# A four-layer network on one core: attention weights times values in one part of sixteen, a fourth weights buffer, the end in halves, and a new table of orders

## The reference, cut to what matters

```python
q, k: 16 heads of 32; v: 8 heads of 64
dots = einsum('bhqd,bhkd->bhqk', q, k)
attn_w = softmax(dots, axis=-1).reshape(B, H, 2, T, T)
attn_w = attn_w[:, :, 0] - lam * attn_w[:, :, 1]
attn = einsum('bhqk,bhkd->bhqd', attn_w, v)
...
rms = sqrt(mean(attn * attn, axis=-1, keepdims=True))
attn = gamma * (attn / (rms + EPS)) * (1.0 - LAMBDA_INIT)
return attn.transpose(0, 2, 1, 3).reshape(B, T, 2 * H * D) @ Wout
```

## Time and profile before

| what | value |
|---|---|
| runs: median (lowest, highest) of 3 | 2716.16 us (2714.27, 2717.32) |
| the profiled execution's own time | 2715.86 us |
| its span, first to last instruction | 2713.5 us |
| granted TensorE clock, mean over the span | 0.898 |
| busy in the span: PE, DVE, ACT, POOL | 79%, 77%, 64%, 57% |
| attention stage | 1026.5 to 2064 us of the span |

### The profile page before, as it was taken

How to read it: one execution, slowest core, us unless ns; L and a number is a source line. 1 busy time by engine, 2 the same in 40 slices (tenths; PEclk the granted TensorE clock), 3 DMA queues, 4 the chain that set the end, 5 groups by cost and what they waited for, 6 DMA issues and landing times.

```text
span 2713.5 us, 42415 instructions
## 1 busy us (share of the span) xinstructions
PE 2148.9 (79%) x15570; PEld 1464.3 (54%) x15570; DVE 2101.5 (77%) x3554; ACT 1741.9 (64%) x2750; POOL 1547.5 (57%) x1375
## 2 busy tenths in 40 slices
PE   2433896797696997898989898889996699769886
PEld 1101564465364674565666566556664568546675
DVE  6999899899886218999999999999998432762344
ACT  6443886786674538898888888888894234222432
POOL 1545335434534006788877987898788524673156
PEclk7555898899798998999999999999998899879988
DMA  2000000000000101111101110111110000000000
GB/s 115 0 0 0 1 1 1 1 1 20 1 1 1 24 1 24 25 25 25 26 23 30 29 27 21 28 24 25 24 36 24 1 1 1 1 16 1 1 1 16
DMA packets 22093, 42.22 MB, mean 16 GB/s; under 512 B 6528, under 2 KB 7040, under 8 KB 21504
## 3 DMA queue, kind: packets, MB, share of 16 engines
q1 hardware_dynamic: 21888, 39.52, 5.5%
HBM read 12.23 MB, written 2.10 MB: 5 GB/s over the span
## 4 chain that ended last, share of the span: by engine, by line
PE 36%; DVE 29%; issue 13%; ACT 12%; POOL 10%; DMA 0%; POOLq 0%; ACTq 0%; DVEq 0%
DVE MA L1326 12%; PE ps L888 6%; DVE WB L1335 5%; PE ps L817 3%; ACT HR L789 3%; PE ps L1187 2%; PE ps L1158 2%; PE ps L819 2%; PE ps L818 2%; PE ps L2048 2%; ACT BIG L455 2%; PE ps L1170 2%; POOL MA L421 2%; PE ps L1990 2%; ACT L789 1%
## 5 line engine op out<-in xcount | busy, mean ns | idle before, releaser
L1326 DVE TENSOR_REDUCE MA<-ps 128x1 f32<-128x1024 f32 x512 | 606.5, 1215 | 43.9 <-PE ps L1158 39.5
L1254 ACT ACTIVATE WB<-ps,MA 128x1024 f32<-128x1024 f32 x461 | 513.3, 1117 | 107.7 <-DVE MA L1326 95.9
L421 POOL TENSOR_TENSOR MA<-MA,BIG 128x1024 f32<-128x1024 f32 x128 | 303.1, 2388 | 475.0 <-DVE BIG L343 450.5
L1158 PE MATMUL ps<-BIG 96*128 96x512 f16 x1024 | 314.1, 389 | 100.7 <-ACT WB L1254 90.1
L1410 POOL TENSOR_SCALAR WB<-WB,MA 128x384 f32<-128x384 f32 x256 | 370.7, 1448 | 8.5
L888 PEld LDWEIGHTS ps<-WB,HR 128*128 128x128 f32 x2304 | 273.5, 192 | 32.4 <-issue 10.5
L888 PE MATMUL ps<-WB,HR 128*128 128x128 f32 x2304 | 282.4, 278 | 9.6 <-DVE acc L724 9.6
L1766 POOL TENSOR_TENSOR BIG<-MA,BIG 128x512 f32<-128x512 f32 x128 | 133.2, 1048 | 237.1 <-PE ps L2034 87.1
L789 ACT ACTIVATE HR<-ps,second 128x512 f32<-128x512 f32 x288 | 189.7, 686 | 113.4 <-PE ps L819 112.4
L1170 PE MATMUL ps<-first,WB 128*128 128x128 f32 x1640 | 225.7, 282 | 1.1 <-ACT WB L1261 0.4
L1413 POOL TENSOR_TENSOR WB<-WB 128x384 f32<-128x384 f32 x205 | 209.1, 1020 | 17.1
(11 more groups left out here) (314 smaller groups left out, 4933.2 us busy)
## 6 DMA issues: line engine op xcount, KB each, us to landing
BIG<-BIG SPq DMA_DIRECT2D x192, 64.0 KB, 2.0
BIG<-MA SPq DMA_DIRECT2D x192, 64.0 KB, 2.0
WB<-w_dram SPq DMA_DIRECT2D x1, 2304.0 KB, 15.0
X<-x_dram SPq DMA_DIRECT2D x4, 512.0 KB, 16.2
HR<-w_dram SPq DMA_DIRECT2D x1, 2048.0 KB, 9.6
out_dram<-X SPq DMA_DIRECT2D x4, 512.0 KB, 2.6
BIG<-wqkv_dram SPq DMA_DIRECT2D x1, 1536.0 KB, 6.2
WB<-w_dram SPq DMA_DIRECT2D x2, 512.0 KB, 5.1
```

What stands on the lines that cost most here:

```text
L421: e.tensor_tensor(yy[:, c, :], yy[:, c, :], db[n % 2][c], ALU.add).then_inc(*p_my.up(b, n, c))
L1158: x = e.matmul(ps[s][:, 512 * h:512 * h + 512], stack[q % 2][0:96, 0, 2 * pp + s, 128 * i:128 * i + 128], stack[q % 2][0:96, 1, 2 * pp + s ...
L1254: e.activation(P_of(n, s), ps[s][:, :], ACT.Exp, bias=L[:, 2 * s + pp:2 * s + pp + 1], scale=1.0, accum_out=L[:, 4 + 2 * s + pp:5 + 2 * s ...
L1326: e.tensor_reduce(L_of(n)[:, c:c + 1], ps[s][:, :], AX, ALU.max, negate=True).then_inc(*v_amx.up(n, s))
```

## The change

It makes no arithmetic different. It has five parts.

1. `weigh0` emits nothing, and `weigh1` emits all sixteen products of a pair and carries the one semaphore increment. `t_aw` has one tick per pair.
2. The second map gets a fourth buffer. It lies in a tile `spread` of 128 x 1024; `combT`, which had 9 partitions of its own, becomes its first nine.
3. The end of a round is a stream of its own (`end_dve`, `end_pool`) in halves of four tiles: the first half may start after step 7 of the last experts. `store` writes 256 KB pieces.
4. `LATE` has a number for each kind of piece instead of `between`, and for some steps one number for even units and one for odd.
5. All tables of due times get new numbers (`IN_AT0` to `A_AT`, `LATE`, `D_AT`; not shown, except for `LATE`).

```diff
+        spread = sb("spread", [128, 1024])
+        combT = spread[0:9, :]
...
-        LATE = {"pe": {"scores1": -0.12, "flip0": -0.01, "flip1": -0.37, "weigh0": 0.71, "weigh1": 0.06,
-                       "settle": 0.03, "between": -0.22},
+        LATE = {'pe': {'scores0': (-0.07, 0.08), 'scores1': (-0.11, 0.05), 'flip0': (-0.16, -0.18), 'flip1': (-0.29, -0.34), 'weigh0': 0.73, 'weigh1': -0.01, 'settle': 0.02, 'norm': -0.22, 'turn': -0.33, 'op': -0.26, 'v': -0.03, 'a3': -0.17, 'a4': -0.23},
...
-              [WB[:, 1024 * i:1024 * i + 1024] for i in range(3)]]
+              [WB[:, 1024 * i:1024 * i + 1024] for i in range(3)] + [spread[:, :]]]
...
-                if part == 0:
+                if part == 1:
                     e.wait_ge(*a_at.at(n))
...
-                for k in range(4 * part, 4 * part + 4):
+                for k in range(8 * part):
                     for pp in range(2):
                         x = e.matmul(bank[6][64 * pp:64 * pp + 64, 0:128], V[(4 * b + g) % 2][:, k, 64 * pp:64 * pp + 64],
                                      DT[(2 * m + pp) % 4][:, 128 * k:128 * k + 128], start=k == 0, stop=k == 7)
-                x.then_inc(*t_aw.up(m, part))
+                if part:
+                    x.then_inc(*t_aw.up(m))
...
+        def end_dve(e, k):
+            for r in range(2):
+                hs = (s_hs[k], s_hs1[k])[r]
+                for h in range(2):
+                    tiles, s = hs[:, 4 * h:4 * h + 4, :], st[f"d{k}"][:, 4 * h:4 * h + 4, :]
+                    yield end_at(k, r, h, "end_stats")
+                    stats(e, s, [tiles[:, j, :] for j in range(4)], {0: p_dm[k].at(r, 8 * h + 7)}).then_inc(
+                        *v_dend[k].up(r, h, "stats"))
+                    yield end_at(k, r, h, "end_norm")
+                    e.wait_ge(*p_dend[k].at(r, h))
+                    norms(e, s, [tiles[:, j, :] for j in range(4)], tiles, range(4)).then_inc(*v_dend[k].up(r, h, "out"))
```

More of the change, by code:

```diff
@@ L290, in rstd @@
             e.wait_ge(*pool_own.now())
-            return e.tensor_tensor(s[:, 0:n, 9:10], s[:, 0:n, 8:9], half_col[0], ALU.pow)
+            return e.tensor_tensor(s[:, 0:n, 9:10], s[:, 0:n, 8:9], half_col[0][:, 0:n, :], ALU.pow)
         def stats(e, s, src, ready):
-            for j in range(8):
+            for j in range(len(src)):
                 if j in ready:
@@ L996, in at @@
                 t, p = ORDER[x]
-                what = p[0] + str(p[2]) if p[0] in ("scores", "flip", "weigh") else p[0] if p[0] in UNIT_AT else "between"
-                return round(t + LATE[engine].get(what, 0), 3) if p[0] != "end" else t
+                late = LATE[engine].get(p[0] + str(p[2]) if p[0] in ("scores", "flip", "weigh") else p[0], 0)
+                if isinstance(late, tuple):
+                    late = late[p[1] % 2]
+                return round(t + late, 3) if p[0] != "end" else t
             return [(at(x), ORDER[x][1]) for x in sorted(range(len(ORDER)), key=lambda x: (at(x), x))]
@@ L1484, in program @@
         a_dg = two("a_dg", *keys(16))
-        v_dln = two("v_dln", *keys((2, 3), ("stats", "out")))
+        v_dln, v_dend = two("v_dln", *keys((2,), ("stats", "out"))), two("v_dend", *keys(2, ("stats", "out")))
         v_dop = two("v_dop", *keys(("stats0", "out0", "stats1", "out1", "sumsq")))
@@ L1784, in soft_pool, with end_pool @@
                                     s_sc[k][x % 2].rearrange("p (j c) -> p j c", c=128), ALU.add).then_inc(*p_dm[k].up(r, x))
-                yield d_at(k, r, "stats3")
-                root(r, 3)
-                yield d_at(k, r, "norm3")
-                e.wait_ge(*v_dln[k].at(r, 3, "out"))
-                xb = X[:, 8 * b:8 * b + 8, :]
-                e.tensor_tensor(xb, xb, hs, ALU.add).then_inc(*p_dx[k].up(r))
+        def end_pool(e, k):
+            for r in range(2):
+                b, hs = k + 2 * r, (s_hs[k], s_hs1[k])[r]
+                for h in range(2):
+                    yield end_at(k, r, h, "end_stats")
+                    e.wait_ge(*v_dend[k].at(r, h, "stats"))
+                    rstd(e, st[f"d{k}"][:, 4 * h:4 * h + 4, :], 4).then_inc(*p_dend[k].up(r, h))
+                    yield end_at(k, r, h, "end_x")
+                    e.wait_ge(*v_dend[k].at(r, h, "out"))
+                    xb = X[:, 8 * b + 4 * h:8 * b + 4 * h + 4, :]
+                    e.tensor_tensor(xb, xb, hs[:, 4 * h:4 * h + 4, :], ALU.add).then_inc(*p_dx[k].up(r, h))
         def open_pool(e, k):
@@ L2094, in store @@
         def store(e):
-            for b in range(NB):
-                e.wait_ge(*p_dx[b % 2].at(b // 2))
-                e.dma_start(out[128 * b:128 * b + 128, :], X[:, 8 * b:8 * b + 8, :].rearrange("p j c -> p (j c)")).then_inc(
-                    s_o, 16)
-            e.wait_ge(s_o, 16 * NB)
+            for r in range(2):
+                for h in range(2):
+                    for k in range(2):
+                        b = k + 2 * r
+                        e.wait_ge(*p_dx[k].at(r, h))
+                        e.dma_start(out[128 * b:128 * b + 128, 512 * h:512 * h + 512],
+                                    X[:, 8 * b + 4 * h:8 * b + 4 * h + 4, :].rearrange("p j c -> p (j c)")).then_inc(s_o, 16)
+            e.wait_ge(s_o, 16 * 2 * NB)
         def over(f, e):
```

62 lines of the change are left out of this document (28 added, 34 removed).

## The result

| | before | changed |
|---|---|---|
| median of 4 runs each | 2716.74 us | 2735.27 us |
| lowest, highest | 2714.27, 2718.32 | 2732.41, 2738.92 |
| span of the profiled execution | 2713.5 us | 2730.4 us |
| ratio | | 1.007, 95% interval 1.0052 to 1.0087 |

The change makes the kernel slower by 0.7%, where 1.6% was forecast. The span grew by 16.9 us. Three readings of the two profiles split it. The first row maximum of the attention starts at 1031.9 us, not at 1020.5: +11.4. From the first maximum to the end of the last one it takes 1050.5 us, not 1042.0: +8.5. Behind the last maximum 648.0 us are left, not 651.0: -3.0.

The account below looks back on a forecast made before the run. Attention was taken as bound by VectorE, 95% busy, and equally by a 6.88 us loop over scores of ps0. Span 2713.5 + 54 (attention) - 6 (end) - 5 (tables) = 2756.5, so 2759 us, range 2690 to 2795.

Parts of the forecast that it names:

- a loop over the scores of ps0: Attention, TensorE to VectorE to ScalarE and back: 6.88 us, the pair's whole length; anything coming into it is paid.
- the gap: TensorE, from scores of ps0 to scores of ps1 in the even unit: grows from 2.60 to 3.30 us.
- ScalarE's part: Waiting gathering copy and copy of the transposes delay ScalarE's exponentials: loop closes at 7.7 us instead of 7.58.
- the price of the new table in front: Mamba and first experts reordered: -5 us, bounds -20 and +15, taken together with the last stage.
- Pairs with a projection or values: Attention pairs with an eviction on ScalarE: 8.35 us each, 90 pairs, 751.5 us.
- What comes on top: Attention above the loop: batch ends 16 us, layernorm pairs 21, first pair's fill, first layernorm and last pair 15.
- The fourth buffer: ScalarE's wait for a POOL difference in attention: zero gain, at best -5 us in the batch ends.
- The end in halves: After the experts' last step: 10.5 us instead of 18.6, so -8; 2 charged for first halves among steps, net -6.
- the attention's lower bound: Attention stage's smallest growth, with batch ends at VectorE's work alone: +46 us, against +54 forecast.
- B: Rival, chance 0.15: the sixteen products cost no time where they stand; kernel faster, 2693 us.
- D: Rival, chance 0.10: VectorE's work stays, so no change; only the end's halves show, 2710 to 2716 us.
- C: Rival, chance 0.10: TensorE waits more per pair, its granted clock falls; dearer, 2793 us at half the fall to 0.88.

Follow-up runs that it names:

- h3: The changed kernel with ScalarE's gathering copy put back behind the exponential of ps0; 2738.46 us in one run.
- h4: The changed kernel with all eight transposes of the even unit behind the scores of ps1; 2732.15 us in one run.
- f1: The kernel before with the fourth buffer for the second map and nothing else; 2720.05 us, ratio 0.9996.
- f2: The kernel before with the end in halves alone, all orders ahead of it as before; 2711.92 us, ratio 0.9969.
- e3: The changed kernel with the nine tables of Mamba, first experts and attention's opening as before; 2727.11 us, ratio 1.0023 to the kernel before.
- e2: The kernel before with one part of sixteen products at the second part's place, all else as before; 2812.92 us, ratio 1.0352.

## Why the prediction was wrong

The direction held, and so did the mechanism, a loop over the scores of ps0 into which the sixteen products come. The size did not: 43 us more than before were forecast, 2759, and 19 were measured, 2735. The step that failed is the length of the pairs, "90 pairs at 8.35 = 751.5 and 38 at 7.7 = 292.6, together 1044". By the rows they take 7.92, 7.95 and 7.43, together 996. Two terms went into that, the gap and ScalarE's part, and the price of the new table in front had the wrong sign besides. In terms of the span, 2756.5 was forecast and 2730.4 measured, 26.1 less: attention 45.5 less, the front 16 more (11.4 measured, -5 taken for it and the last stage together), the end 3 more.

**The gap.** 3.30 was forecast, 3.14 measured. The mis-sized term is the 1.03 in "the gap becomes 2.60 + 1.03 - 0.33": eight products behind eight others cost 0.87, not the 1.03 between the first of eight and the next matmul. Sixteen take 1.89 in the rows above, and 1.03 + 0.87 is 1.90. Over 128 pairs the 0.16 are some 20 us.

**ScalarE's part of the loop.** The prediction closed it at 7.7, by the copy ending at 1.02 and the exponentials behind it. The row shows an exponential 0.93 behind the start of such a copy, and the loop closes at 7.43 by the four times alone. That the gathering copy waits for all products costs nothing (h3: pairs stay at 7.43). That the copy of the transposes is a second path just as long was right (h4: 7.38 without the gap).

**Pairs with a projection or values.** This is the term that was mis-sized most: 90 pairs at 8.35. The prediction added durations, copy 1.02 and eviction 0.61. From start to start they are 0.92 and 0.48 in the rows of the pair above, 0.23 less, and the gap's 0.16 comes on top; the pair is 7.92. Pairs in which values are evicted take 7.95. With the same counts, 38 x 7.43 + 60 x 7.92 + 30 x 7.95 = 996, where the prediction had 1044. These 48 us are more than the whole 45.5 by which the stage was forecast too long.

**What comes on top.** 52 us were forecast above the loop; 1050.5 - 996 = 54.5 were measured. That this agrees is partly luck. The five pairs at each batch end have 4.9 above the loop (44.0, with one pair at 7.43 and four at 7.92), where 5.2 was taken. The last pair takes 8.8 and not the old 14.6, which the prediction had kept. So some 9 us more than forecast lie in the rest; the pairs behind a layernorm, 9.06 us each above, are part of it, and it was not followed further.

Against the kernel before the dense pairs lost 29.5 us, while the three batch ends won 15.6 and the last pair 5.8 (table). Of the 15.6 the prediction had 7.5, by its 46.3 for five pairs at an end.

**The fourth buffer**: zero in the kernel before, as said (f1).

**The end in halves**: 9.9 us from the last step on. The prediction said 10.5, but its parts add up to 10.9, or to 9.7 if the second statistics stand beside the first root; the root over half the columns, for which it took 1.67, is 1.04 in the rows above. The whole part is worth 8 us (f2), with the forecast 6 inside f2's interval. In the one profile of the changed kernel only 3 of it show, since the stage ahead of it varies from execution to execution by as much.

**The front.** "-5, bounds -20 and +15" had the wrong sign: +11.4 in this profile, 10 over all profiles. VectorE's idle time there bounded what could be won and said nothing of what could be lost (e3).

**The range.** The prediction gives the attention's lower bound as +46 in one place and as +40 in another; its own sum has +46. The forecast does not hang on it, and neither bound reaches down to the 8.5 measured.

**The rivals.** B (faster, the products hidden) falls: e2 shows that they are paid in full in the old order. D (no change, since VectorE's work stays) falls too: the kernel is slower beyond its interval, and VectorE's busy time even fell, by 27 us. VectorE was busy 95% before, and a loop through three engines, as long as its work, decided. The Trainium skill (Perfetto Trace Analysis, Identifying the Most-Contended Engine) takes the engine with the highest occupancy as the one to optimize first. Here that is VectorE before (95%) and after (91%), and this share alone does not tell of the loop. C (TensorE's clock) is not what happened in the change, whose granted clock in the stage is 0.98, but it is a part of what happened in e2 (0.94).

## What to carry to other kernels

Add up a loop from start to start, not from durations: back-to-back instructions on ScalarE start a tenth of a microsecond before the profiled end of the one ahead here (a copy of 1.02 us, the next start after 0.92), and over 128 pairs that was about half of the 48 us. When an order of work is changed together with the size of a step, price the step in both orders, and the irregular places (batch ends, first and last repeat) apart from the regular ones. If a pair has two loops, move work so that both are nearly equal: in the new order four and twelve beat eight and eight and sixteen. Keep the old order as a rival: with it, eight and eight were shorter still.
